# Clearing the expert slots during the time mix, in 1 MB transfers, instead of during the channel mix

## The reference

```python
h = layernorm(x) * (1 + ca) + sa
# RWKV block: time mix, then channel mix
a = layer_norm(h); aa = time_shift(a)
k, v, r = mix(a, aa, m) @ W.T            # three 512x512 products
h = h + (sigmoid(r) * wkv(k, v)) @ Wo.T
a = layer_norm(h); aa = time_shift(a)
kv = silu(mix(a, aa, cm_mk) @ Wkey.T) @ Wval.T      # 512 -> 2048 -> 512
h = h + sigmoid(mix(a, aa, cm_mr) @ Wcr.T) * kv
x = x + ga * h
# mixture of experts: 2 shared experts, 16 routed ones, the best 2 per token
h = layernorm(x) * (1 + cb) + sb
gate = top-2 of softmax(h @ W_router)
x = x + gb * (shared(h) + sum over experts of gate * down(gelu(up(h))))
```

## Time and profile before

| what | value |
|---|---|
| median of three runs | 1025.0 us (1024.59 to 1025.46) |
| the profiled execution's own time | 1022.83 us |
| its span | 1021.1 us |
| mean granted clock of TensorE | 0.95 |
| PE busy | 905.6 us, 89% of the span |
| DVE, ACT, POOL busy | 514.4, 383.2 and 398.0 us |
| share of the 16 DMA engines taken by SP's and ACT's queue | 43.0% |

### The profile page before, as it was taken

One profiled execution on the slowest core, in us unless ns is written; L12 is line 12 of the kernel. 1 busy time (PEld: TensorE's weight loads), 2 busy tenths in 40 slices (PEclk: granted clock), 3 DMA queues, 4 the chain that ended last, 5 costly groups with the idle time before them and its releaser, 6 DMA issues.

```text
span 1021.1 us, 13501 instructions
## 1 busy us (share of the span) xinstructions
PE 905.6 (89%) x4254; PEld 728.0 (71%) x4255; DVE 514.4 (50%) x873; ACT 383.2 (38%) x630; POOL 398.0 (39%) x309
## 2 busy tenths in 40 slices
PE   7897889999989996999999999999892899999950
PEld 2465678787768885888888878888671788878740
DVE  5896988985762111521351144117663344444377
ACT  2664573856446331222222122444231333333331
POOL 3332100000123462115014101863477989886174
PEclk9899989999979998999999999999996999999985
DMA  8515423231445268149226942637787677668487
GB/s 351 167 42 166 140 86 106 71 115 42 137 152 176 92 197 236 45 148 274 80 93 197 288 144 103 196 114 242 264 318 289 190 269 231 215 225 286 155 243 230
DMA packets 116784, 181.64 MB, mean 178 GB/s; under 512 B 10216, under 2 KB 55272, under 8 KB 115968
## 3 DMA queue, kind: packets, MB, share of 16 engines
q1 hardware_dynamic: 106272, 145.37, 43.0%
q0 software_dynamic: 10464, 35.66, 10.8%
HBM read 106.23 MB, written 74.76 MB: 177 GB/s over the span
## 4 chain that ended last, share of the span: by engine, by line
PE 62%; DVE 11%; DMA 7%; POOL 6%; issue 6%; SPq 5%; ACT 3%; DVEq 0%; ACTq 0%; POOLq 0%
PE kk_ps L395 5%; PE kk_ps L396 5%; PE kk_ps L397 5%; PE kv_ps L397 4%; PE kv_ps L395 4%; PE kv_ps L396 4%; SPq L542 4%; PE mm_ps L395 4%; PE mm_ps L396 4%; PE mm_ps L397 4%; PE up_ps L395 4%; POOL xs_s L2311 3%; PE up_ps L396 3%; PE up_ps L397 3%; PE dn_ps L395 2%
## 5 line engine op out<-in xcount | busy, mean ns | idle before, releaser
L1535 DVE TENSOR_TENSOR silu<-kk_ps,silu 128x512 fp32r<-128x512 f32 x64 | 44.3, 692 | 248.1 <-ACT silu L2084 248.1
L395 PE MATMUL kk_ps<-xk,cm_w 128*128 128x512 f32 x256 | 103.4, 404 | 10.8 <-DVE xk L1576 10.8
L2080 ACT ACTIVATE kk_ps<-kk_ps 128x512 f32<-128x512 f32 x64 | 37.2, 582 | 191.9 <-PE kk_ps L397 191.9
L396 PE MATMUL kk_ps<-xk,cm_w 128*128 128x512 f32 x256 | 101.5, 397 | 0.0
L397 PE MATMUL kk_ps<-xk,cm_w 128*128 128x512 f32 x256 | 101.3, 396 | 0.0
L397 PE MATMUL kv_ps<-cm_w,silu 128*128 128x512 f32 x256 | 99.8, 390 | 0.0
L396 PE MATMUL kv_ps<-cm_w,silu 128*128 128x512 f32 x256 | 99.7, 390 | 0.0
L395 PE MATMUL kv_ps<-cm_w,silu 128*128 128x512 f32 x256 | 99.7, 389 | 0.0
L2273 POOL TENSOR_TENSOR rs<-mv,neghalf 128x1 f32<-128x1 f32 x16 | 15.5, 968 | 169.8 <-DVE mv L1557 169.8
L2238 POOL TENSOR_TENSOR rs<-mv,neghalf 128x4 f32<-128x4 f32 x12 | 14.0, 1163 | 158.3 <-DVE mv L1264 158.2
L2231 POOL TENSOR_TENSOR cm_w<-stage,cm_w 128x1024 fp32r<-128x1024 f32 x16 | 38.6, 2419 | 93.2 <-ACT cm_w L1895 93.2
(11 more groups left out here) (227 smaller groups left out, 2340.6 us busy)
## 6 DMA issues: line engine op xcount, KB each, us to landing
xs_s<-zero SPq DMA_DIRECT2D x52, 256.0 KB, 3.7
stage<-in_wex POOLq DMA_DIRECT2D x26, 512.0 KB, 4.6
xsb<-xs_s SPq DMA_DIRECT2D x44, 256.0 KB, 3.1
ys_s<-ysb SPq DMA_DIRECT2D x41, 256.0 KB, 2.5
stage<-in_wcm SPq DMA_DIRECT2D x16, 512.0 KB, 3.9
wmod<-in_wmod SPq DMA_DIRECT2D x6, 1024.0 KB, 11.7
stage<-in_wtm SPq DMA_DIRECT2D x10, 512.0 KB, 6.2
ys_s<-zero SPq DMA_DIRECT2D x20, 256.0 KB, 3.7
```

The costliest lines, as they stand in the source:

```text
L395: pe.matmul(out, lhs[0], rhs[0], start=first, stop=False)
L396: pe.matmul(out, lhs[0], rhs[1], start=False, stop=False)
L1535: dve.tensor_tensor(silu[:, g % NSILU, 1, :], kk_ps[g % 2][:, :], silu[:, g % NSILU, 0, :].bitcast(F32), ALU.subtract).then_inc(s_silo, 1)
L2080: act.activation(kk_ps[g % 2][:, :], kk_ps[g % 2][:, :], ACT.Silu).then_inc(s_silu, 1)
```

## The change

All clears (72 of 256 KB before, 18 MB together) are issued as 18 transfers of 1 MB (four neighbouring tiles of slots, 13 for `xs_s` and 5 for `ys_s`), six in each of the batches 0, 1 and 2 of the time mix. There they stand on SP's list after the store of `xk` of the batch before and the load of x, and ahead of `store_sr(b - 1)`, `store_x2(b, [0])` and `load_h0(b, [2])`. The source is the same tile `zero`, now read 16 times over for each partition; a partition writes 8 KB of device memory in one piece instead of 2 KB. The two waits for `s_zero` are for a quarter of the count.

```diff
             def clear_slots(i):
 
-                n = -(-NSX // (NB - 1))
+                groups = [(xs_s, q) for q in range(0, NSX, 4)] + [(ys_s, q) for q in range(FULL, NSX, 4)]
+                n = len(groups) // (NB - 1)
                 sp.wait_ge(s_con, 1)
-                for q in range(i * n, min(NSX, (i + 1) * n)):
-                    for rows_s in (xs_s, ys_s):
-                        if rows_s is xs_s or q >= FULL:
-                            sp.dma_start(rows_s[q * P:(q + 1) * P, :].rearrange("p (k c) -> p k c", k=KT),
-                                         zero[:, :].rearrange("p (k c) -> p k c", k=1).to_broadcast([P, KT, P]))\
-                                .then_inc(s_zero, 16)
+                for rows_s, q in groups[i * n:(i + 1) * n]:
+                    sp.dma_start(rows_s[q * P:(q + 4) * P, :].rearrange("(p r) h -> p (r h)", p=P)
+                                 .rearrange("p (k c) -> p k c", c=P),
+                                 zero[:, :].rearrange("p (k c) -> p k c", k=1).to_broadcast([P, 4 * KT, P]))\
+                        .then_inc(s_zero, 16)
...
                 if b == NB - 1:
                     load_half(10, cm_half(10))
                     load_half(11, cm_half(11))
+                if b + 1 < NB:
+                    clear_slots(b)
                 if b:
                     store_sr(b - 1, [0] if b == NB - 1 else range(TT))
                 store_x2(b, [0])
...
             load_base(0, [2, 3])
-            clear_slots(0)
             load_xk(1)
...
                 if b + 1 < NB:
-                    clear_slots(b)
                     load_xk(b + 1)
...
-            sp.wait_ge(s_zero, 16 * (2 * NSX - FULL))
+            sp.wait_ge(s_zero, 16 * (2 * NSX - FULL) // 4)
...
-            pool.wait_ge(s_zero, 16 * (2 * NSX - FULL))
+            pool.wait_ge(s_zero, 16 * (2 * NSX - FULL) // 4)
```

## The result

The changed kernel takes 1041.26 us in the median (1039.12 to 1045.14, four runs), the kernel before beside it 1025.23 us: a ratio of 1.0166 (95% interval 1.0145 to 1.0188), slower by 16.0 us. (The ratios here are worked out from the single executions, with the few that ran in a slower state left out, and are not quite the quotient of the two medians.) The profiled execution took 1045.14 us, its span is 1043.4 us.

A forecast was written before the change was run, and what follows sets the result against it. PE, busy 89% of the span, was taken to bound the kernel. Losses of 11.9, 15.1 and 10.9 us less a gain of 15.9 made +22.0 us, on 1025.0 a forecast of 1047 us, range 1031 to 1058.

The forecast's parts named there:

- all four places: The channel mix, where time is gained, and batches 0, 1 and 2 of the time mix, where it is lost.
- The gain of 15.9 us: Channel mix: without clears ahead of the xk loads, PE gains 11.6 us in batch 1 and 4.3 in batch 3.
- A megabyte of clears takes 3.63 us: DMA engines set the pace whatever the transfer size: 3.63 us per MB, 21.8 us for six.
- Batch 0, 11.9 us: Time mix: the h0 load behind the clears lands at about 119.3 us, so DVE's O tile 2 loses 11.9 us.
- Batch 1, 15.1 us: Time mix: the first sr store behind the clears lands late, holding ACT's sigmoid; DVE and PE lose about 15.1 us.
- Batch 2, 10.9 us: Time mix, quiet DMA engines: the sr store lands at 233.8 us and DVE's low part loses 10.9 us.
- The sum: Time mix 38 us longer; less the channel mix gain, +22.0 us in all.
- The span: Whole kernel: profiled span of 1021.1 + 22.0 = 1043.1 us.
- SP's time in the clears, 21 us: Time mix: SP would be in the clears for about 21 us in each of three batches.
- the larger clears are not faster: Denies the rival that 1 MB transfers run faster, giving back up to 17.3 us: 1030 us; chance 0.14 for 1034 or less.
- The clears are not passed by: Denies the rival that small transfers go through between the clears' pieces in the time mix: 1009 to 1018 us; chance 0.05.

The follow-up runs named there:

- e3: Changed kernel with its 18 transfers of 1 MB moved back to the channel mix, six at each of the three old places; 1042.68 us against 1035.51, ratio 1.0067.
- e10: The kernel before, unaltered, run and profiled again; 1031.97 us against 1032.58, ratio 1.0001.
- e2: Changed kernel with the clears at the same places but in pieces of 256 KB, 24 per batch; 1052.65 us against 1035.51 for the kernel before, ratio 1.0136.
- e7: Changed kernel with POOL issuing the same 18 transfers on its own queue, ahead of its second-norm step; 1020.53 us against 1025.20 for the kernel before, ratio 0.9946.
- e4: Changed kernel with three of each batch's six transfers moved behind the last store of x2; 1020.94 us against 1035.51 for the kernel before, ratio 0.9867.
- e5: Changed kernel with all six transfers per batch four lines down, behind the last store of x2; 1021.54 us against 1035.51 for the kernel before, ratio 0.9886.

## Why the prediction was right, and where it was off

The direction, the mechanism and all four places were right; the forecast was +22.0 us and the measured difference +16.0.

- *The gain of 15.9 us.* Right: 363.7 - 347.8 = 15.9 us. e3 shows the same term from the other side. Its two parts, 11.6 and 4.3 us, were read from one execution and don't repeat as well as their sum: in e10 the 18th product of batch 1 starts at 409.2 us, 9.9 us late and not 11.6, while the stage as a whole loses 15.6.
- *A megabyte of clears takes 3.63 us.* Right: 284 to 292 GB/s in the three blocks, DMA share 1.03 to 1.04. e2 shows that the size of a transfer doesn't matter by more than 2 us in all.
- *Batch 0, 11.9 us.* Measured as 10.5 us on DVE. The load lands at 117.9 and not at 119.3.
- *Batch 1, 15.1 us.* Mis-sized, 12.7 us. This is the largest error. The mechanism is as predicted, ACT waits 15.47 us for the store of sr. The store lands 25.1 us after SP reaches the clears (161.46 to 186.6); I had 27.5. I let the clears start only when all of x had been moved. They share the engines: in 161 to 163 us the share is only 0.74, and from 163 to 165 the mixture moves 329 GB/s. The same holds for batch 0, with 28.4 us in place of 29.6.
- *Batch 2, 10.9 us.* Measured as 10.4. With nothing in the engines before it the time to the landing is 24.7 us against the 25.0 forecast.
- *The sum.* The first `kv_ps` product comes 33.9 us later (319.3 to 353.2); I had 37.9. With the gain the last `kk_ps` product is 18.0 us later, forecast 22.0. All of the miss in the mixes is these 4 us.
- *The span.* 1043.4 us against the 1043.1 forecast is luck: 18.0 us of effect and 4.3 us by which the end of this execution was longer than that of the execution before. The medians differ by 16.0 us, 2 us less than the mixes, which is within what the end varies by.
- *SP's time in the clears, 21 us.* Wrong by 1 to 4 us (20.0, 17.8, 17.4), without effect, since the next transfer lands when the clears are through, whenever it was issued.

The rivals: the larger clears are not faster, by the rate in the blocks and by e2 and e3; the rule of the Trainium skill on transfers of 1 MiB ("DMA: Bandwidth & Descriptors", section "Rules for kernel authors") had nothing to give here, where the engines were at a share of 1.03 with pieces of 256 KB already. The clears are not passed by: the first store of sr lands 25 us after SP's arrival, 0.7 us after the last clear. The rule on order within a ring (same page, section "Queues, rings and completion order") agrees with the trace, and e7 adds, by one load in batch 0, what a second queue does here: it takes away the wait for the whole block and leaves that for a share of the engines. e4 shows that a loss is the drain time less the slack of its place, not a share of the bytes: with 21.8 us to drain, the losses of 10.5, 12.7 and 10.4 us leave a slack of 11, 9 and 11, and half the clears (10.9 us) lose 1.6 us in batch 1 and nothing in the others. e5 shows that with enough slack the loss is nothing.

## What to carry to other kernels

A bulk transfer costs what stands behind it on the same list, less the slack of the first item that is needed; so look at the next transfers and their deadlines, not at the average load of the stage. Here the DMA engines had room in the time mix as a whole, the same call four lines further down cost nothing, and three transfers instead of six at the bad place cost nearly nothing. A reader of a two-buffer store (ACT for `srb`) has a deadline too, although stores look as if nobody waited for them.

## What was not expected of the hardware

- SP gets past transfers of 1 MB sooner than past the same bytes in pieces of 256 KB, and the next transfer lands later after its issue. In batch 2 six transfers of 1 MB take SP 17.4 us, the 24 of 256 KB in e2 take 21.0. The page's issues of the changed kernel, against the earlier trace rows:

```profile
xs_s<-zero SPq DMA_DIRECT2D x13, 1024.0 KB, 9.4
...
ys_s<-zero SPq DMA_DIRECT2D x5, 1024.0 KB, 10.2
```

  At 3.6 us per MB some 2.6 MB are on their way, an estimate from these rows, where 3.7 us for a small clear meant 1 MB. The store of sr behind them takes 7.27 us to land (179.34 to 186.61), in e2 3.5 us. No run here shows what sets this depth.
- How many products are slow after a stall differs with the execution. Of the 18 products of batch 1 of the channel mix 13 are slow after gaps of 7.1 and 1.2 us, all 18 after 12.3 and 1.2 us (e3), but only 6 after 6.8 and 1.2 us in the second profile of the kernel before (e10):

```profile
406.44 0.47 PE L395 MATMUL kk_ps<-xk,cm_w 128*128 128x512 f32 x1 [1.22 <-ACT xk L2076]
406.74 0.40 PE L396 MATMUL kk_ps<-xk,cm_w 128*128 128x512 f32 x1
```

  From 406 to 409 us the granted clock is 1.00 there and 0.50 in the first profile. So a stall costs more than its own length, but not by an amount that one profile gives.
- The part behind the channel mix, which no edit here touches but for the count of a wait, takes 338 to 357 us by chip and execution (the kernel before alone 338 and 349); a pair of spans is not enough for an effect of 0.5%.
